# Start and pace of the indirect gathers in a graph layer: which are free at the start, and how often the next is handed over

## The chip, the cores and the metric

One core of one Trainium2 chip runs the whole kernel. The metric is the device time in microseconds (us) of one execution; the median of several runs is compared.

## The reference

The input has 12,500 nodes with 128 features each, and 200,000 edges (source, destination), sorted by destination.

```
h   = maximum(layernorm(x), 0)
agg = segment_sum(h[src], dst) / maximum(deg, 1)
h1  = relu(agg @ Wg + h @ Ws + bg)
h2  = tanh(h1 @ W1 + b1)          # 128 -> 512
h3  = tanh(h2 @ W2 + b2)          # 512 -> 512
out = x + h3 @ W3 + b3            # 512 -> 128
```

## The kernel before

The nodes are cut into 49 blocks of 256. First x is normalized in five chunks; the result is split into a high and a low float16 half, kept in SBUF (`tab`) and written to a table in DRAM (`h_table`). Then the blocks' neighbour sums are made in two ways.

Blocks 0 to 22 ("pool" blocks) are summed from a ring in SBUF. GpSimd issues 744 indirect DMAs, one for each tile of 128 edges, numbered here 0 to 743; each fetches 128 rows of the table into the next of 64 places of the ring (line 638). TensorE multiplies the ring's tiles with one-hot matrices (line 712), 18 tiles for each step of 128 nodes; there are 46 steps, 0 to 45. Before step s, `begin_sums(s)` waits until gathers 0 to 16s + 23 have landed and reads a lead with `value_load`.

Blocks 23 to 48 ("units", 26 of them, 0 to 25) use no gather. For each unit VectorE and TensorE sort the edges into groups (`place_edges`, `count_groups`, `rank_edges`, `spread_ranks`; matmuls of `place_chunk`, line 760, whose result ScalarE copies to `q_sb`, line 1127). TensorE turns the result (line 769), ScalarE copies it to `qlT` (line 1133), and SP writes it to DRAM and spreads it over all partitions (lines 563 and 565, 1.6 MB): these are the unit's codes. VectorE compares the codes with partition numbers (`match_codes`, line 1480), TensorE picks the messages in 25 "pairs" of four matmuls each (`gather_pairs`, line 787), ScalarE copies each pair (line 1113), and `sum_unit` (line 803) adds them up. VectorE's order is written out by hand: at the start it is `rank_edges(0)`, `spread_ranks(0)`, `place_edges(1)`, `count_groups(1)`, `take_nodes(0)` (line 1499, needs `q_sb`), `split_sources(1)`, a memset, and `match_codes(0)`. SP's queue at the start holds the loads of the first three blocks' own rows and then the codes of units 0 and 1.

The dense layers (line 815 and 818 for layer 1, 824, 841, 858 for the others) of one block are interleaved by hand with the pairs of one unit and the sums of two steps. A period takes one pool block and one unit; there are 25 periods, of which 1, 2 and 13 have no pool block's layers.

GpSimd's gathers are released in three ways. The first FIRST_LOTS = 12 wait only for the table. From gather 12 on, the unit 0 codes' `qlT_ready` must have come. From gather OPEN_LOTS = 24 on, each waits for one more increment of `lot_free`. TensorE gives these increments: at each matmul, while the program is built, `pace(mm, ns)` adds an assumed duration to a clock, and if that clock has reached `due` and the ring has a free place, this matmul increments `lot_free`; `due` then moves on by LOT_NS = 1400. These nanoseconds are constants in the code, not measured times. A "lot" is one gather (LOT = 1). After the last step's tiles are in, nothing more is gathered.

Of the kernel before, what the change touches and what calls it, by code (L numbers as in the profile page):

```python
# [35 lines left out]
RING = RG * GT  # L36
RW = 258
LOT = 1
FIRST_LOTS = 12
OPEN_LOTS = 24  # L40
LOT_NS = 1400
BLK = 256
SUB = 128
W = 18
# [25 lines left out]
def at(eng, sem, value):  # L70

    if not isinstance(value, int) or value > 0:
        eng.wait_ge(sem, value)


def wait_alone(eng, sem, value, passed):

    eng.wait_ge(sem, value)
    eng.sem_inc(passed)


def gnn_program(nc, x, src, dst, Wg, Ws, bg, W1, b1, W2, b2, W3, b3, out):
# [61 lines left out]
    with ExitStack() as ctx:  # L144
# [280 lines left out]
        def chunk_rows(c):  # L425

            return TP, ROWS, xin[:, c * ROWS:(c + 1) * ROWS]
# [5 lines left out]
        def table_whole(eng):  # L433
            for s in range(2):
                eng.wait_ge(table_in[s], 16 * len(SPREAD) * ((TC + 1 - s) // 2))
# [14 lines left out]
        def over_all_tiles(eng, m, step):  # L450

            step(0, m * TILES + 1)
            with eng.Fori(1, TILES - 1) as t:
                step(t, m * TILES + t + 1)
            step(TILES - 1, (m + 1) * TILES)

        def is_general(eng):
            eng.wait_ge(general_ready, 1)
            return eng.value_load(general[0:1, 0:1], min_val=0, max_val=1) > 0
# [140 lines left out]
        @block.gpsimd  # L600
        def _(pool):
            nc.gpsimd.memset(ident[:], 0.0).then_inc(ident_zero, 1)
            pool.wait_ge(ident_zero, 1)
            nc.gpsimd.affine_select(out=ident[:], in_=ident[:], compare_op=ALU.not_equal, fill=1.0, base=0,
                                    pattern=[[-1, P]], channel_multiplier=1).then_inc(ident_ready, 1)
            nc.gpsimd.iota(iota, pattern=[[1, BLK]], base=0, channel_multiplier=0,
                           allow_small_or_imprecise_dtypes=True).then_inc(iota_ready, 1)
            pool.wait_ge(ident_ready, 1)
            nc.gpsimd.tensor_copy(ident16[:], ident[:]).then_inc(ident_ready, 1)
            nc.gpsimd.iota(threshold[:], pattern=[[0, 1]], base=0, channel_multiplier=SUB,  # L610
                           allow_small_or_imprecise_dtypes=True).then_inc(iota_ready, 1)
            nc.gpsimd.iota(base_tab[:, 0:STEPS], pattern=[[SUB, STEPS]], base=0, channel_multiplier=0,
                           allow_small_or_imprecise_dtypes=True).then_inc(iota_ready, 1)
            nc.gpsimd.iota(base_tab[:, STEPS:SUBS], pattern=[[SUB, SUBS - STEPS]], base=STEPS * SUB - 1, channel_multiplier=0,
                           allow_small_or_imprecise_dtypes=True).then_inc(iota_ready, 1)
            nc.gpsimd.iota(first_row, pattern=[[16, SUBS]], base=-15, channel_multiplier=0,
                           allow_small_or_imprecise_dtypes=True).then_inc(iota_ready, 1)

            for c in range(TC):
                s = c % 2  # L620
                p, rows, held = chunk_rows(c)
                at(pool, pair_ready, c - 1)
                pool.wait_ge(shift_ready, c + 1)
                for r in range(POOL_ROWS):
                    ins = nc.gpsimd.tensor_scalar(hval[0:p, s, r, 0:D], held[0:p, r], scale[0:p, s, r:r + 1],
                                                  shift[0:p, s, r:r + 1], ALU.mult, ALU.add)
                ins.then_inc(pool_scaled, 1)

            table_whole(pool)
            pool.wait_ge(turned, 2 * TB)  # L630

            pool.wait_ge(idx_turned, TB)

            def gather_lot(d):

                for t in range(LOT * d, LOT * (d + 1)):
                    k = t // GT % RG
                    nc.gpsimd.indirect_dma_start(  # L638
                        out=ring_tiles[:, t % RING, 0:2 * D], out_offset=None, in_=table,
                        in_offset=bass.IndirectOffsetOnAxis(ap=idx_all[:, t:t + 1], axis=0),  # L640
                    ).then_inc(gathered[k], 16)

            for d in range(LOTS):
                if d == FIRST_LOTS:
                    pool.wait_ge(qlT_ready, 1)
                elif d >= OPEN_LOTS:
                    wait_alone(pool, lot_free, d - OPEN_LOTS + 1, issuing)
                gather_lot(d)

            with pool.If(is_general(pool)):  # L650
                def gather_tile(t, n):
                    wait_alone(pool, gen_idx_ready, n, issuing)
                    nc.gpsimd.indirect_dma_start(
                        out=ring_tiles[:, 0, 0:2 * D], out_offset=None, in_=table,
                        in_offset=bass.IndirectOffsetOnAxis(ap=general_idx[:, 0:1], axis=0),
                    ).then_inc(gen_gathered, 16)

                with pool.Fori(0, BLOCKS) as m:
                    pool.sem_inc(gen_counting)
                    over_all_tiles(pool, m, gather_tile)  # L660

                    wait_alone(pool, gen_seg, (m + 1) * TILES, issuing)
                    pool.inc_swdge_sem([gen_gathered], [16 * TILES], mode="sub")

        @block.tensor
        def _(pe):
# [22 lines left out]
            def pace(mm, ns, tells=False):  # L689

                lots["clock"] += ns
                free = min(LOTS, lots["summed"] + LOTS_HELD) - lots["given"] - OPEN_LOTS
                if lots["clock"] >= lots["due"] and free > 0 and not tells:
                    lots["given"] += 1
                    lots["due"] = max(lots["due"] + LOT_NS, lots["clock"] + LOT_NS * 3 // 4)
                    mm.then_inc(lot_free, 1)

            def begin_sums(s):

                assert lots["given"] + OPEN_LOTS >= STEP_LOTS * s + (2 * GT + GT) // LOT  # L700
                at(pe, mean_done, s)
# [148 lines left out]
            def layer4(k, carried=0, beside=None, paced=True):  # L850

                at(pe, oblk_ready, k)
                at(pe, carry_taken, carried)
                for t in range(NT):
                    for q in range(HC):
                        if t == 0 and q in (0, HC - 1):
                            pe.wait_ge(h3_ready, HC * k + (HC if q else HC - 1))
                        mm = nc.tensor.matmul(out_ps[:, t], h3T[:, q, t * P:(t + 1) * P], w3[:, q],  # L858
                                              start=(q == 0), stop=(q == HC - 1))
                        if paced:  # L860
                            pace(mm, 215, t == NT - 1 and q == HC - 1)
                        if t == NT - 1 and q == HC - 1:
                            mm.then_inc(l4_done, 1)
                        if beside:
                            beside(HC * t + q)
# [143 lines left out]
            layer4(LAST_UNIT)  # L1009
            assert lots["given"] == LOTS - OPEN_LOTS  # L1010

# [722 lines left out]
```

## Time and profile before

| | us |
|---|---|
| median of 3 runs | 1424.96 |
| lowest and highest | 1423.08 to 1429.42 |
| the profiled execution | 1426.06 |
| its span, first to last instruction | 1424.1 |
| TensorE matmuls busy | 1238.2 (87%) |
| VectorE busy | 1085.5 (76%) |
| GpSimd busy | 754.2 (53%) |
| ScalarE busy | 628.0 (44%) |

The times in the profile are those of one execution, counted from its first instruction. An engine's idle time is shown before the instruction that ended it, with what released it; "issue" and "remote" mean that no instruction of this core was found as releaser. Ends of matmuls are modelled, their starts are recorded.

### The profile page before, as it was taken

Reading aid. Unit: us, or ns where it says so; the run is one execution under the profiler, and the core shown is the slowest. Engines: PE = TensorE matmul, PEld = TensorE weight load, DVE = VectorE, ACT = ScalarE, POOL = GpSimd, SP = SyncE. Lnnn points to the kernel's source line nnn. Section 1 sums busy time; section 2 is a strip of 40 time slices with the busy share of each in tenths; the row PEclk is TensorE's granted clock in tenths of the full one; section 3 lists DMA queues with packets and bytes.
Section 4 is the critical chain, followed back from the end, with each engine's and each line's share of the span. In section 5 each row is a group of like instructions: output and inputs, shape, how many; then the busy total and the mean of one; then the engine's idle time right before and its main releaser. Section 6 shows DMA issues by size and latency. Waiting matters only on the chain.

```text
span 1424.1 us, 28546 instructions
## 1 busy us (share of the span) xinstructions
PE 1238.2 (87%) x10196; PEld 942.0 (66%) x10196; DVE 1085.5 (76%) x2058; ACT 628.0 (44%) x1297; POOL 754.2 (53%) x796
## 2 busy tenths in 40 slices
PE   0327888999999999999989989999999999999988
PEld 0114666776776777777766767777767777777767
DVE  8787899678778868868867886886787788788641
ACT  6513455345435435435525543553453354354342
POOL 3274644555555555555545555555555565555530
PEclk9658999999999999999999999999999999999999
DMA  9632412441441342342233225324414414423410
GB/s 236 220 111 80 96 45 77 104 110 40 107 109 52 99 104 63 85 107 83 66 101 96 81 63 107 87 62 109 105 44 107 111 44 103 109 65 82 112 32 11
DMA packets 88769, 129.02 MB, mean 91 GB/s; under 512 B 45329, under 2 KB 71271, under 8 KB 84055
## 3 DMA queue, kind: packets, MB, share of 16 engines
q1 hardware_dynamic: 64825, 78.37, 20.5%
q0 software_dynamic: 23808, 48.81, 14.1%
q8 instruction: 88, 1.44, 0.4%
q14 instruction: 48, 0.39, 0.1%
HBM read 107.53 MB, written 13.16 MB: 85 GB/s over the span
## 4 chain that ended last, share of the span: by engine, by line
PE 74%; DVE 8%; issue 6%; ACT 5%; another core or an unknown queue 4%; DMA 3%; DVEq 0%; SPq 0%; POOL 0%; POOLq 0%; ACTq 0%
PE banks L841 22%; PE banks L787 21%; PE banks L803 8%; PE banks L858 6%; PE banks L712 6%; PE banks L824 4%; DVE arena L1490 3%; PE banks L760 2%; ACT arena L1113 2%; DMA xin<-in_x_dram 2%; PE banks L818 2%; PE banks L815 2%; ACT dense L1096 1%; DVE arena L1480 1%
## 5 line engine op out<-in xcount | busy, mean ns | idle before, releaser
L638 POOL DMA_INDIRECT ring<-h_table,idx_all x744 | 732.5, 984 | 588.9 <-issue 221.6
L1113 ACT CAST arena<-banks 128x512 f16<-128x512 f32 x650 | 366.0, 589 | 192.3 <-PE banks L787 141.6
L787 PE MATMUL banks<-xin,arena 125*128 125x256 f16 x2600 | 371.7, 276 | 63.5 <-issue 26.6
L841 PE MATMUL banks<-dense,w 128*128 128x256 f32 (+1 forms) x1568 | 419.0, 384 | 8.7 <-ACT dense L1096 4.7
L787 PEld LDWEIGHTS banks<-xin,arena 125*128 125x128 f16 x2600 | 236.7, 98 | 164.0 <-issue 80.8
L841 PEld LDWEIGHTS banks<-dense,w 128*128 128x128 f32 x1568 | 265.7, 191 | 47.3 <-ACT dense L1096 13.4
L1490 DVE TENSOR_TENSOR arena<-node,banks 128x768 f16<-128x768 f16 x208 | 191.5, 981 | 22.0 <-PE banks L803 21.5
L1480 DVE TENSOR_SCALAR arena<-arena,code_ptr 128x768 f16<-128x768 f16 (+1 forms) x416 | 177.6, 489 | 17.8 <-PE banks L787 14.9
L803 PE MATMUL banks<-arena 64*128 64x257 f16 x2600 | 162.1, 271 | 5.7 <-DVE arena L1490 3.4
L712 PE MATMUL banks<-ring,onehot 128*128 (+1 forms) x828 | 158.5, 274 | 1.1 <-issue 0.2
L1103 ACT ACTIVATE dense<-banks,b2c 128x256 f32<-128x256 f32 (+1 forms) x196 | 93.6, 479 | 130.6 <-PE banks L841 113.2
L803 PEld LDWEIGHTS banks<-arena 64*128 64x128 f16 x2600 | 119.1, 94 | 46.7 <-issue 18.5
L1339 DVE TENSOR_TENSOR onehot<-iota,banks 128x2304 f16<-128x2304 f16 x46 | 117.5, 2554 | 1.6
L824 PE MATMUL banks<-dense,w 128*128 128x256 f32 (+1 forms) x392 | 109.5, 396 | 8.0 <-ACT dense L1088 8.0
L1551 DVE TENSOR_TENSOR dense<-banks,xblk 128x256 f32<-128x256 f32 x49 | 20.8, 425 | 123.2 <-issue 60.4
L858 PE MATMUL banks<-w,dense 128*128 128x128 f32 x784 | 111.4, 283 | 2.9 <-DMA ring<-h_table,idx_all 1.7
L712 PEld LDWEIGHTS banks<-ring,onehot 128*128 128x128 f16 x828 | 78.7, 97 | 52.4 <-issue 14.2
L1096 ACT ACTIVATE dense<-banks,b1c 128x256 f32<-128x256 f32 (+1 forms) x196 | 81.9, 470 | 65.9 <-PE banks L824 55.4
L858 PEld LDWEIGHTS banks<-w,dense 128*128 128x128 f32 x784 | 100.0, 191 | 14.2 <-issue 9.3
L1433 DVE TENSOR_TENSOR arena<-arena,banks 128x1800 f16<-128x1800 f16 x52 | 102.9, 2021 | 0.1
L1088 ACT ACTIVATE dense<-banks,bgc 128x256 f32<-128x256 f32 (+1 forms) x49 | 23.2, 474 | 164.4 <-PE banks L818 153.5
L824 PEld LDWEIGHTS banks<-dense,w 128*128 128x128 f32 x392 | 67.8, 196 | 21.5 <-ACT dense L1088 15.3
(123 smaller groups left out, 862.8 us busy)
## 6 DMA issues: line engine op xcount, KB each, us to landing
arena<-unit_codes SPq DMA_DIRECT2D x26, 1600.0 KB
ring<-h_table,idx_all POOLq DMA_INDIRECT x744
xblk<-in_x_dram SPq DMA_DIRECT2D x48, 128.0 KB
out_dram<-dense SPq DMA_DIRECT2D x48, 128.0 KB
xin<-in_x_dram SPq DMA_DIRECT2D x5, 1120.0 KB
h_table<-xin SPq DMA_DIRECT2D x5, 1120.0 KB
own_pair<-h_table SPq DMA_TRANSPOSE x98
w<-in_L_gnn_W_dram SPq DMA_DIRECT2D x1, 1024.0 KB, 11.5
```

Source lines behind the costliest of these rows:

```text
L638: nc.gpsimd.indirect_dma_start(out=ring_tiles[:, t % RING, 0:2 * D], out_offset=None, in_=table, in_offset=bass.IndirectOffsetOnAxis(ap=id ...
L712: mm = nc.tensor.matmul(main_ps[:, 0:2 * D + 1], onehot[:, s % 2, j, :], ring_column(window_slot(s, lead, j)), start=(j == 0), stop=(j == ...
L787: mm = nc.tensor.matmul(to, wide_l[0:TP, piece % WSLOTS, k, j, :], tab[0:TP, row_of(g, j), :], start=(j == 0), stop=(j == 1))
L803: mm = nc.tensor.matmul(unit_ps[h][:, 0:2 * D + 1], wide[h * HALF:(h + 1) * HALF, (NP + p) % WSLOTS, g - lo, 0:P], unit_msgs[h * HALF:(h + ...
L824: mm = nc.tensor.matmul(l2_ps[c][:, 0:w], w1[:, c * P:(c + 1) * P], h1T[:, 0:w], start=True, stop=True)
L841: mm = nc.tensor.matmul(l3_ps[c][:, 0:w], w2[:, q, c * P:(c + 1) * P], h2T[:, q, 0:w], start=(q == 0), stop=(q == HC - 1))
L858: mm = nc.tensor.matmul(out_ps[:, t], h3T[:, q, t * P:(t + 1) * P], w3[:, q], start=(q == 0), stop=(q == HC - 1))
L1113: nc.scalar.copy(unit_msgs[:, 2 * pr:2 * pr + wide_of, 0:2 * D], unit_ps[pr % 2][:, 0:wide_of * 2 * D].rearrange("p (g d) -> p g d", d=2 * ...
L1339: nc.vector.tensor_tensor(onehot[:, b], iota16[:].unsqueeze(1).to_broadcast([P, W, P]), held.unsqueeze(2).to_broadcast([P, W, P]), ALU.is_ ...
L1433: ins = nc.vector.tensor_tensor(oh_pay[:, :, k], hits[:, :, 0:HI], place_ps[:, 1 + k].unsqueeze(2).to_broadcast([P, UT, HI]), ALU.mult)
L1480: ins = nc.vector.tensor_scalar(wide_l[:, p % WSLOTS, 0:hi - lo, j, :], codes[:, lo * P:hi * P].rearrange("p (g w) -> p g w", w=P), code_p ...
L1490: nc.vector.tensor_tensor(wide[:, (NP + p) % WSLOTS, 0:hi - lo, 0:P], node16[:, 0:P].unsqueeze(1).to_broadcast([P, hi - lo, P]), qd_ps[:, ...
```

## The change

The first gather of all now waits for `qlT_ready`, the copy that unit 0's codes are written from. Only 14 gathers are then free in place of 24; every later one is handed over by TensorE's `pace`, whose interval is 1375 in place of 1400 ns. FIRST_LOTS is gone. The number of increments rises from 720 to 730.

```diff
-FIRST_LOTS = 12
-OPEN_LOTS = 24
-LOT_NS = 1400
+OPEN_LOTS = 14
+LOT_NS = 1375
...
             for d in range(LOTS):
-                if d == FIRST_LOTS:
+                if d == 0:
                     pool.wait_ge(qlT_ready, 1)
-                elif d >= OPEN_LOTS:
+                if d >= OPEN_LOTS:
                     wait_alone(pool, lot_free, d - OPEN_LOTS + 1, issuing)
                 gather_lot(d)
```

## Rows read from the trace of the kernel before

**Rows 1.** First section of the page: busy us, share of the span, instructions.

```profile
PE 1238.2 (87%) x10196; PEld 942.0 (66%) x10196; DVE 1085.5 (76%) x2058; ACT 628.0 (44%) x1297; POOL 754.2 (53%) x796
```

**Rows 2.** Groups by line: busy, mean ns, idle before and its releaser.

```profile
L638 POOL DMA_INDIRECT ring<-h_table,idx_all x744 | 732.5, 984 | 588.9 <-issue 221.6
...
L712 PE MATMUL banks<-ring,onehot 128*128 (+1 forms) x828 | 158.5, 274 | 1.1 <-issue 0.2
```

**Rows 3.** Timeline of GpSimd at the start: start, duration, idle before.

```profile
71.78 1.14 POOL L638 DMA_INDIRECT ring<-h_table,idx_all  x1 [20.85 <-DMA h_table<-xin]
...
85.93 1.34 POOL L638 DMA_INDIRECT ring<-h_table,idx_all  x1 [0.30 <-issue]
90.61 1.22 POOL L638 DMA_INDIRECT ring<-h_table,idx_all  x1 [3.35 <-ACT qlT L1133]
...
112.32 0.94 POOL L638 DMA_INDIRECT ring<-h_table,idx_all  x1 [0.31 <-issue]
116.14 0.95 POOL L638 DMA_INDIRECT ring<-h_table,idx_all  x1 [2.87 <-PE banks L787]
```

**Rows 4.** Timeline of TensorE's matmuls at the start.

```profile
82.09 0.96 PE L760 MATMUL banks<-arena 128*64 128x100 f16 x18 [0.30 <-DVE arena L1458]
...
99.95 7.15 PE L787 MATMUL banks<-xin,arena 125*128 125x256 f16 x36 [9.91 <-DVE arena L1480]
108.92 0.60 PE L787 MATMUL banks<-xin,arena 125*128 125x256 f16 x4 [1.82 <-issue]
110.29 0.61 PE L787 MATMUL banks<-xin,arena 125*128 125x256 f16 x4 [0.77 <-issue]
113.83 1.04 PE L787 MATMUL banks<-xin,arena 125*128 125x256 f16 x4 [2.93 <-issue]
116.05 1.01 PE L787 MATMUL banks<-xin,arena 125*128 125x256 f16 x4 [1.19 <-ACT arena L1113]
...
117.28 8.98 PE L787 MATMUL banks<-xin,arena 125*128 125x256 f16 x48
126.94 1.01 PE L760 MATMUL banks<-arena 128*64 128x100 f16 x36 [0.68 <-ACT arena L1113]
...
135.00 0.28 PE L712 MATMUL banks<-ring,onehot 128*128 128x257 f16 x1
```

**Rows 5.** Timeline of ScalarE at the start.

```profile
89.27 0.24 ACT L1127 COPY q_sb<-banks 128x100 f32<-128x100 f32 x1 [17.46 <-remote]
...
113.19 0.59 ACT L1113 CAST arena<-banks 128x512 f16<-128x512 f32 x1 [2.96 <-remote]
...
127.99 0.24 ACT L1127 COPY q_sb<-banks 128x100 f32<-128x100 f32 x1 [1.10 <-PE banks L760]
```

**Rows 6.** Timeline of VectorE at the start.

```profile
86.48 0.37 DVE L1413 TENSOR_TENSOR arena<-arena 128x400 f16<-128x400 f16 x1
89.55 0.21 DVE L1499 COPY banks<-q_sb 128x50 f32<-128x50 f32 x1 [2.69 <-ACT q_sb L1127]
...
97.47 0.10 DVE L1664 MEMSET arena<- 128x50 f16 x1 [0.24 <-DVE code_all L1328]
98.82 2.96 DVE L1480 TENSOR_SCALAR arena<-arena,code_ptr 128x768 f16<-128x768 f16 x8 [1.25 <-DMA arena<-unit_codes]
```

**Rows 7.** Chain that ended last, in order of time: start, us, what.

```profile
90.37 1.29 DMA unit_codes<-qlT
91.67 6.64 DMA arena<-unit_codes
...
1371.33 2.51 DMA ring<-h_table,idx_all
```

**Rows 8.** Timeline of TensorE's matmuls, end of the last two periods.

```profile
1321.04 0.59 PE L818 MATMUL banks<-dense,wg 128*128 128x256 f32 x2
...
1372.49 0.59 PE L818 MATMUL banks<-dense,wg 128*128 128x256 f32 x2
1374.84 0.68 PE L858 MATMUL banks<-w,dense 128*128 128x128 f32 x4 [1.75 <-DMA ring<-h_table,idx_all]
```

## The prediction

> **What bounds the kernel now.** The page's first section comes first: TensorE is busy 1238.2 of 1424.1 us and GpSimd, which only issues the gathers, 754.2 [rows 1]. The middle of the kernel is matmul after matmul, so a change of the gathers can pay only where TensorE sits idle. Next the groups by line: the 744 gathers stood idle 588.9 us in total, so GpSimd is not the limit, and the matmuls that read the gathered tiles (L712) lost 1.1 us to waiting [rows 2]. That leaves the timeline at the two ends of the gather stream, engine by engine.
>
> The head. GpSimd issues gathers 0 to 11 in one run from 71.78 to 85.93, waits for unit 0's codes, and issues 12 to 28 in a second run to 112.32; from 116.14 on it waits for matmuls [rows 3]. Beside the first run, the 36 matmuls of place_chunk(0) end at 82.09 + 0.96 = 83.05, yet ScalarE's copy of their result starts at 89.27, after 17.46 us of waiting [rows 4, 5]. For unit 1 the same pair of steps has no gap: matmuls end at 126.94 + 1.01 = 127.95, copy at 127.99. So **6.2 us** are lost before 89.27. Beside the second run TensorE's pairs lose 1.82 + 0.77 + 2.93 + 1.19 = **6.7 us** between 107 and 116 [rows 4], and ScalarE's cast at 113.19 waited 2.96 us [rows 5] though its matmuls, pair 9's, ended at 108.92 + 0.60 = 109.52. Once gathers are paced, 48 matmuls take 8.98 us from 117.28 without a gap [rows 4]. Late completions thus lie beside long gather runs. Against that, the first 36 pair matmuls (pairs 0 to 8), 7.15 us from 99.95, lie in the second run and have no such gap.
>
> The tail. Step 45 needs the very last gather, issued at 1371.33 and landed 2.51 us later [rows 7]. TensorE had ended layer 1 at 1372.49 + 0.59 = 1373.08 and starts at 1374.84: **1.75 us** idle [rows 8].
>
> **The change part by part.**
>
> *First gather behind unit 0's codes.* Nothing is queued behind the waiting gather on GpSimd but other gathers. It empties 71.8 to 90 of twelve gathers. If these caused the 6.2 us, ScalarE's copy starts at 83.1. What is late next is VectorE: it finishes count_groups(1) at 86.48 + 0.37 = 86.85; take_nodes(0), split_sources and the memset took 89.55 to 97.57, 8.02 us [rows 6], so they would end at 94.9. The codes, 6.2 us earlier on SP, would land at 91.67 + 6.64 - 6.2 = 92.1 [rows 7] and no longer matter. match_codes(0) then starts at 95.0 in place of 98.82 [rows 6]: **-3.8 us**, not 6.2. The cover for the other 2.4 is VectorE's own work.
>
> Here a rule speaks against the gain. The trace shows a late completion beside gathers, no mechanism [rows 3, 4]. The Trainium skill, "SBUF — State Buffer", section "Who interferes with whom", says a DMA never contends with a compute engine. By it the 6.2 us stay, and the sum loses its 3.8. The first-run gap speaks against this rule here and the 36 undisturbed matmuls for it.
>
> *14 free in place of 24, all others handed over.* The run after the codes is 14 gathers, plus those that pace() has handed over by then. Adding up pace()'s own ns along TensorE's program: gathers 14 and 15 go in place_chunk(0), then one each 1375 ns, which is 3 pairs. Gathers cost 1.26 us each (85.93 - 71.78 over 11, 1.29) [rows 3]; from 84.4 on, gather 14 is reached at 102.4 and 20 at 110, when pair 14 (the one that hands it over) is due at 96.1 + 14 x 0.8 = 107 (0.8 is 7.15 over 9 pairs) [rows 4]. So the long run now ends at about 110 after 20 gathers, in place of 29, but still lies beside the pairs. The 6.7 us can vanish (-6.7), stay (0) or grow (D). The row nearest to the new order is the old second run itself, which had the loss: I take 0.
>
> Ten more gathers wait for a semaphore; paced and unpaced ones are both issued 0.30 us after the last when free [rows 3], so this costs 0.
>
> Is the ring filled in time? Step 0 needs gather 23. By the same adding up it is handed over at 12.5 us of pace clock, in pair 23 of unit 0, near 117.28 + 8.98 - 0.6 = 125.7 today. With 0.95 to issue and at most 2.51 to land it is there at 128.3; step 0 starts at 135.00 [rows 4, 7]. Both ends move together, so 6.7 us are spare: cost 0, and if that cover is gone, its excess. Step 1 needs gather 39, handed over at 34.9 us of pace clock where the step begins at 46.8: also 0.
>
> *1375 in place of 1400 ns.* At step 43 the last gather needed is handed over at 1026.2 us of pace clock before and 1011.4 after; for step 45 it is 1073.4 and 1057.8, of 1075.1 when the step begins. Between those steps, layer 1 ends move from 1321.04 to 1372.49, 51.45 us, for 44.7 of pace clock, so 15.6 is 18 us of time [rows 8]. The last gather would be in the ring about 16 us before its use: **-1.75 us**, all of it on the path, since only matmuls follow. Nothing else waits there; no gain is to be had at other steps, where L712 hardly waits [rows 2]. The steeper pace adds no DMA bytes.
>
> Sum: -3.8 - 1.75 = -5.55 on an execution of 1426.06 (span 1424.1 and 2.0 around it), 1420.5. The three times have their median at 1424.96, 1.1 below, so the median after is **1419.4**, 0.39% less.
>
> **Rivals.**
>
> A (forecast, 0.40): as above, 1419.4.
>
> B (0.25): both losses come from long runs of gathers, and the shorter second run takes away its loss too. For it: the pairs from 117.28 on are clean as soon as gathers are paced. Against: 20 gathers in a row remain beside or before them. 1424.96 - 5.55 - 6.7 = 1412.7.
>
> C (0.20): the first gap isn't the gathers' doing, so the change does nothing at the head; tail gain only, 1423.2. For it: the ends of matmuls are the profile's model, and pairs 0 to 8 ran undisturbed beside gathers. Against: units 0 and 1 run the same 36 matmuls and only one is late. On this the Trainium skill, "Perfetto Trace Analysis", section "Tensor Engine Instruction (MATMUL, LD_WEIGHTS)", says the end shown for a matmul is an estimate and the semaphore follows PSUM's acknowledgement; taken alone it would leave the gap unexplained but real, at C's time.
>
> D (0.10, slower): the run now begins ten gathers before the pairs, and holds TensorE's completions from the first pair until about the run's end, as the first run held place_chunk(0)'s until 89.27, 2 us after its last gather. Sixteen gathers from 84.4 are issued by 104.6 and landed by 107. Pair 12 would then start at 107 + 11 x 0.8 = 115.8, against 116.05 today: the head's gain is gone but for 0.2. If the last three of today's gaps come on top, 0.77 + 2.93 + 1.19 = 4.9 are lost: 1424.96 - 0.2 + 4.9 - 1.75 = 1427.9. It is slower than before once pair 12 starts later than 116.05 + 1.75 = 117.8. Gather 23 would have to be 6.7 us late to add to this.
>
> The rest (0.05): small shifts of the phases of the periods, either way, 2 us.
>
> **How the numbers follow.** The three times spread over 6 us, and 0.5% is 7.1 us: that is what I take as telling a change from none, so faster means below 1417.8, slower above 1432.1. Faster: B, 0.25, and what of A (a partial gain in the pairs, over 1.6 of the 6.7) and the rest falls below the line, 0.09: 0.34. Slower: D prolonged by another 4.2 us or with gather 23 late: 0.06. Same: 0.60. Range: from B less 1.7 us of scatter to between C and D: 1411 to 1426, leaving out D's end and the edges. A's own range is 1417 to 1422.
>
> **What the profile after would show.** Step 1: ScalarE's q_sb copy (L1127) at about 83 and the first gather just after 84; else C. Step 2: VectorE at work without a gap from 82 to 95 and L787 starting near 96. Step 3: gathers back to back up to number 20 or so, then waiting for L787; gaps in L787 of about 6.7 us in total for A, none for B, over 10 for D. Step 4: step 0 starts near 131 with no wait for the ring. Step 5: the last gather near 1350, and L858 of step 45 starts 0.1 to 0.4 us after L818 ends. The prediction is wrong if q_sb's copy stays near 89, or if the middle, from 140 to 1320, changes its length by more than 2 us, where I expect nothing.

## The result, and the profile after

The changed kernel takes **1441.0 us** (median of 11 runs) against 1425.61 us of the kernel before beside it: a ratio of **1.0099, 95% interval 1.008 to 1.0118**. It is slower by 1%, where 1419.4 us, 0.4% faster, was predicted. The ratio leaves out one run of each kernel, 2087.29 us at a granted clock of 0.562, and 1807.06 us. The profiled execution took 1435.4 us, with a span of 1433.5 us; it is 9.3 us longer than the profiled one of the kernel before (1426.06), while the medians lie 15.4 us apart, so the two profiles show some 60% of the loss. In what follows lines of the changed kernel are one lower than before (L786 is the pairs' L787).

First section of the page after, and the groups by line (busy, mean ns, idle before and its releasers):

```profile
PE 1240.8 (87%) x10196; PEld 942.8 (66%) x10196; DVE 1082.7 (76%) x2058; ACT 625.4 (44%) x1297; POOL 746.3 (52%) x796
```

```profile
L786 PE MATMUL banks<-xin,arena 125*128 125x256 f16 x2600 | 370.7, 276 | 84.2 <-ACT arena L1112 39.8 <-DVE arena L1479 23.8 <-issue 17.9
L1112 ACT CAST arena<-banks 128x512 f16<-128x512 f32 x650 | 365.1, 590 | 217.8 <-PE banks L786 178.3 <-issue 21.3 <-remote 12.6
L802 PE MATMUL banks<-arena 64*128 64x257 f16 x2600 | 167.4, 271 | 11.9 <-DVE arena L1489 6.6 <-issue 3.8
L857 PE MATMUL banks<-w,dense 128*128 128x128 f32 x784 | 111.4, 283 | 0.4 <-issue 0.3
```

The busy times are within 8 us of those before [rows 1]. TensorE's idle time grew by 6.8 us, from 1424.1 - 1238.2 = 185.9 to 1433.5 - 1240.8 = 192.7. In the pairs and their casts it grew by more: these two groups had 63.5 us (L787) and 192.3 us (L1113) of it in the kernel before, and have 84.2 and 217.8 now; other groups have less than before.

**The head came out as predicted.** Timelines of ScalarE, VectorE, GpSimd and TensorE at the start (four fences in this order; ... marks lines left out):

```profile
83.05 0.24 ACT L1126 COPY q_sb<-banks 128x100 f32<-128x100 f32 x1 [11.28 <-PE banks L759]
...
110.32 0.59 ACT L1112 CAST arena<-banks 128x512 f16<-128x512 f32 x1 [2.92 <-remote]
```

```profile
86.69 0.20 DVE L1498 COPY banks<-q_sb 128x50 f32<-128x50 f32 x1
...
94.45 0.44 DVE L1479 TENSOR_SCALAR arena<-arena,code_ptr 128x768 f16<-128x768 f16 x1
```

```profile
85.07 1.14 POOL L637 DMA_INDIRECT ring<-h_table,idx_all  x1 [34.78 <-ACT qlT L1132]
...
110.78 0.95 POOL L637 DMA_INDIRECT ring<-h_table,idx_all  x1 [0.31 <-issue]
114.75 1.32 POOL L637 DMA_INDIRECT ring<-h_table,idx_all  x1 [3.02 <-PE banks L786]
```

```profile
82.04 0.96 PE L759 MATMUL banks<-arena 128*64 128x100 f16 x18 [0.30 <-DVE arena L1457]
...
95.50 8.31 PE L786 MATMUL banks<-xin,arena 125*128 125x256 f16 x44 [11.69 <-DVE arena L1479]
105.33 0.61 PE L786 MATMUL banks<-xin,arena 125*128 125x256 f16 x4 [1.52 <-ACT arena L1112]
107.54 1.01 PE L786 MATMUL banks<-xin,arena 125*128 125x256 f16 x4 [1.60 <-issue]
...
110.96 1.03 PE L786 MATMUL banks<-xin,arena 125*128 125x256 f16 x4 [1.99 <-issue]
113.09 1.03 PE L786 MATMUL banks<-xin,arena 125*128 125x256 f16 x4 [1.09 <-issue]
...
131.44 1.74 PE L711 MATMUL banks<-ring,onehot 128*128 128x257 f16 x14
```

The q_sb copy follows its matmuls at 83.05. Twenty gathers run back to back from 85.07 to 110.78. The four gaps in the pairs sum to 1.52 + 1.60 + 1.99 + 1.09 = 6.2 us, where 6.7 us was expected to stay. Step 0 starts at 131.44, 3.6 us before the 135.00 of [rows 4].

**The tail too.** TensorE at the last step: the wait of 1.75 us in [rows 8] is gone.

```profile
1383.27 0.59 PE L817 MATMUL banks<-dense,wg 128*128 128x256 f32 x2
1383.75 0.68 PE L857 MATMUL banks<-w,dense 128*128 128x128 f32 x4
```

**The middle did not.** Start of the last matmul of `sum_unit(n)`, us:

| unit | before | after | difference |
|---|---|---|---|
| 0 | 134.8 | 131.2 | -3.6 |
| 3 | 272.2 | 271.3 | -0.9 |
| 8 | 531.0 | 535.1 | +4.1 |
| 15 | 884.2 | 887.0 | +2.8 |
| 22 | 1242.6 | 1255.2 | +12.6 |
| 24 | 1346.2 | 1358.9 | +12.7 |
| 25 | 1387.6 | 1396.5 | +8.9 |

So 12.7 + 3.6 = **16.3 us** were lost between units 0 and 24, in small pieces: 2.7 to unit 3, 5.0 from there to unit 8, -1.3 to unit 15, 10.0 to unit 24. What a piece looks like, in unit 6 of the changed kernel: GpSimd, then ScalarE.

```profile
393.72 0.95 POOL L637 DMA_INDIRECT ring<-h_table,idx_all  x1 [1.80 <-issue]
394.97 0.95 POOL L637 DMA_INDIRECT ring<-h_table,idx_all  x1 [0.30 <-issue]
396.23 0.95 POOL L637 DMA_INDIRECT ring<-h_table,idx_all  x1 [0.30 <-issue]
397.48 1.13 POOL L637 DMA_INDIRECT ring<-h_table,idx_all  x1 [0.31 <-issue]
398.91 0.95 POOL L637 DMA_INDIRECT ring<-h_table,idx_all  x1 [0.30 <-issue]
400.17 0.95 POOL L637 DMA_INDIRECT ring<-h_table,idx_all  x1 [0.30 <-issue]
```

```profile
394.96 0.59 ACT L1112 CAST arena<-banks 128x512 f16<-128x512 f32 x1 [0.29 <-PE banks L786]
395.83 1.07 ACT L1112 CAST arena<-banks 128x512 f16<-128x512 f32 x2 [0.29 <-PE banks L786]
...
397.96 0.59 ACT L1112 CAST arena<-banks 128x512 f16<-128x512 f32 x1 [0.68 <-PE banks L786]
399.42 0.59 ACT L1112 CAST arena<-banks 128x512 f16<-128x512 f32 x1 [0.88 <-PE banks L786]
400.84 0.59 ACT L1112 CAST arena<-banks 128x512 f16<-128x512 f32 x1 [0.83 <-PE banks L786]
402.29 1.07 ACT L1112 CAST arena<-banks 128x512 f16<-128x512 f32 x2 [0.87 <-PE banks L786]
```

Six gathers run with 0.30 us between them. Before the casts beside the first two ScalarE is idle for 0.29 us, before those beside the later ones for 0.68 to 0.88 us. It looks like the loss of the head again, in small, in the middle.

**Late time.** To add this up I use one measure for all profiles. A pair's late time is the start of ScalarE's cast, less the later of two times: 0.25 us after the start of the pair's last matmul, and 0.53 us after the cast before it. Over 650 pairs it is 121.5 us in the kernel before, with 57 pairs over 0.75 us, and 139.0 us in the changed one, with 76. The difference, 17.5 us, has the size of the loss. Stretch by stretch the two agree only roughly: the late time differs by -1.2 us in units 1 to 3, +11.4 in 4 to 8, +1.9 in 9 to 15 and +6.6 in 16 to 24.

### The profile page after: what moved, and what is told of

Read it like the earlier page. It is cut to its first block, busy times and chain, and to the rows that moved or that the text cites. A ratio compares the mean times of both kernels' runs of the same rounds, so it can differ in the third digit from the quotient of the medians.

```text
span 1433.5 us, 28556 instructions
## 1 busy us (share of the span) xinstructions
PE 1240.8 (87%) x10196; PEld 942.8 (66%) x10196; DVE 1082.7 (76%) x2058; ACT 625.4 (44%) x1297; POOL 746.3 (52%) x796
## 4 chain that ended last, share of the span: by engine, by line
PE 74%; DVE 13%; issue 5%; ACT 4%; DMA 2%; another core or an unknown queue 2%; DVEq 0%; SPq 0%
PE banks L840 22%; PE banks L786 21%; PE banks L802 7%; PE banks L857 7%; PE banks L711 6%; DVE arena L1489 5%; PE banks L823 3%; ACT arena L1112 2%; PE banks L814 2%; DMA xin<-in_x_dram 2%; PE banks L759 2%; PE banks L817 2%; DVE arena L1479 1%; PE banks L736 1%
## 5 line engine op out<-in xcount | busy, mean ns | idle before, releaser
L637 POOL DMA_INDIRECT ring<-h_table,idx_all x744 | 724.6, 974 | 592.9 <-issue 192.2
L1112 ACT CAST arena<-banks 128x512 f16<-128x512 f32 x650 | 365.1, 590 | 217.8 <-PE banks L786 178.3
L786 PE MATMUL banks<-xin,arena 125*128 125x256 f16 x2600 | 370.7, 276 | 84.2 <-ACT arena L1112 39.8
L786 PEld LDWEIGHTS banks<-xin,arena 125*128 125x128 f16 x2600 | 236.3, 98 | 187.1 <-issue 63.6
L802 PE MATMUL banks<-arena 64*128 64x257 f16 x2600 | 167.4, 271 | 11.9 <-DVE arena L1489 6.6
L1550 DVE TENSOR_TENSOR dense<-banks,xblk 128x256 f32<-128x256 f32 x49 | 20.8, 424 | 153.7 <-issue 80.8
L823 PEld LDWEIGHTS banks<-dense,w 128*128 128x128 f32 x392 | 68.8, 199 | 16.9 <-ACT dense L1087 10.1
```

The source lines that it names most:

```text
L637: nc.gpsimd.indirect_dma_start(out=ring_tiles[:, t % RING, 0:2 * D], out_offset=None, in_=table, in_offset=bass.IndirectOffsetOnAxis(ap=id ...
L786: mm = nc.tensor.matmul(to, wide_l[0:TP, piece % WSLOTS, k, j, :], tab[0:TP, row_of(g, j), :], start=(j == 0), stop=(j == 1))
L802: mm = nc.tensor.matmul(unit_ps[h][:, 0:2 * D + 1], wide[h * HALF:(h + 1) * HALF, (NP + p) % WSLOTS, g - lo, 0:P], unit_msgs[h * HALF:(h + ...
L823: mm = nc.tensor.matmul(l2_ps[c][:, 0:w], w1[:, c * P:(c + 1) * P], h1T[:, 0:w], start=True, stop=True)
L1112: nc.scalar.copy(unit_msgs[:, 2 * pr:2 * pr + wide_of, 0:2 * D], unit_ps[pr % 2][:, 0:wide_of * 2 * D].rearrange("p (g d) -> p g d", d=2 * ...
```

## The experiments

Eighteen runs were made, in seven groups; each group shared a chip and its runs of the kernel before. The difference between the chips turned out to be the main thing that they showed. Below, a pair is called late when its late time is over 0.75 us, and a chip is said to have late pairs when its profiles show them. All chips but D were used in one group only, so nothing here tells a trait of the chip from something else that was so at that time, such as work on its other cores; on D all groups gave the same.

| chip | kernel before, us | runs |
|---|---|---|
| that of the result | 1425.61 | the kernels before and after |
| B | 1442.9 | after_1385, before_1375, before_wait_first, after_12_early |
| C | 1324.32 | before_again, after_join, after_pairs_slow, after_pairs_fast |
| D | 1324.2 | before_second, after_second, after_join_second, after_pairs_slow_second |
| D | 1325.03 | no_gathers, after_pairs_slow_third, after_join_third |
| E | 1448.52 | no_gathers_second |
| F | 1323.66 | after_pairs_slow_fourth |
| D | 1324.23 | after_join_fourth |

### Each part alone (chip B)

Three theories are held against each other. P: what counts is which matmuls hand over the gathers. Adding up pace's own ns, 281 of 730 increments sit on a pair's matmul in the changed kernel, 127 of 720 in the kernel before, and 134 of 730 at an interval of 1385. R: the shorter interval itself costs, by its size. F: the late start of the gathers costs. The changed kernel itself did not run on this chip.

**after_1385.**

```diff
-LOT_NS = 1375
+LOT_NS = 1385
```

> The changed kernel with one number altered, LOT_NS 1385 in place of 1375. Adding up pace()'s nanoseconds along the program, 281 of the changed kernel's 730 increments sit on a pair's matmul (127 of 720 before); with 1385 it is 134 of 730, at nearly the same interval and with the same start. Theory P (where the increments fall in the program sets how often a gather is issued beside a pair, and that costs the 13 us of the middle): the middle is as before, the head gain of 3.6 us and the tail gain stay, so 1418 to 1423 and a ratio of 0.995 to 0.999. Theory R (the shorter interval itself costs, by its size): 10 of the 25 ns are given back, ratio 1.005 to 1.007. Theory F (the late start and the emptier ring cost): ratio 1.01 as the changed kernel.

Measured: 1453.33 us, ratio to before 1.0074 [1.0052, 1.0097]. P's forecast fell: with about as few increments on pairs as in the kernel before, it is no faster for it. The interval takes in R's 1.007 and F's 1.01.

**before_1375.** The kernel before with the interval alone:

```diff
-LOT_NS = 1400
+LOT_NS = 1375
```

> The kernel before with only LOT_NS changed to 1375: 24 free, first gather as before; 278 of 720 increments on a pair's matmul. Theory P: the whole middle loss and no head gain, ratio 1.010 to 1.014. Theory R: the same. Theory F: no loss, ratio 0.998 to 1.001 with the tail gain of 1.75 us.

Measured: 1453.35 us, 1.0063 [1.0039, 1.0087]. So on this chip the interval alone costs 0.6%, where F forecast no loss and P and R 1.0 to 1.4%.

**before_wait_first.** The kernel before with the wait moved alone; 24 gathers are free behind the codes:

```diff
-                if d == FIRST_LOTS:
+                if d == 0:
                     pool.wait_ge(qlT_ready, 1)
-                elif d >= OPEN_LOTS:
+                if d >= OPEN_LOTS:
```

> The kernel before with only the wait moved to gather 0 (24 free, 1400 ns kept). Theories P and R: the head gain of 3.6 us and nothing else, ratio 0.996 to 0.999; step 0 starts near 131.4. Theory F: a loss, ratio above 1.003.

Measured: 1451.91 us, 1.006 [1.004, 1.008]. This is the mechanism of rival D of the prediction, in the kernel before. TensorE in unit 0's pairs:

```profile
106.59 0.61 PE L787 MATMUL banks<-xin,arena 125*128 125x256 f16 x4 [2.17 <-issue]
110.22 1.01 PE L787 MATMUL banks<-xin,arena 125*128 125x256 f16 x4 [3.02 <-issue]
...
113.71 1.03 PE L787 MATMUL banks<-xin,arena 125*128 125x256 f16 x4 [2.06 <-issue]
120.05 1.03 PE L787 MATMUL banks<-xin,arena 125*128 125x256 f16 x4 [5.30 <-issue]
129.29 6.00 PE L787 MATMUL banks<-xin,arena 125*128 125x256 f16 x27 [8.22 <-ACT arena L1113]
```

The pairs start 4 us earlier than in [rows 4], and then lose 2.17 + 3.02 + 2.06 + 5.30 + 8.22 = 20.8 us beside one run of 30 gathers, from 85.53 to 123.61, where the kernel before loses 6.7. The last matmul of `sum_unit(0)` starts at 146.1, against 135.8 in before_1375, which starts its gathers as the kernel before does. These 10.3 us at the head are the size of the whole loss, 1451.91 - 1442.9 = 9.0.

**after_12_early.** The changed kernel, with the wait at gather 12:

```diff
-                if d == 0:
+                if d == 12:
                     pool.wait_ge(qlT_ready, 1)
```

> The changed kernel (14 free, 1375 ns) with the wait for unit 0's codes back at gather 12, so that 12 gathers go at once. Theories P and R: the middle loss stays and the head gain goes, ratio 1.011 to 1.014, and the copy of q_sb is back at about 89. Theory F: most of the loss goes, ratio 1.000 to 1.005.

Measured: 1450.05 us, 1.0048 [1.0027, 1.0069]. Its unit 0 is clean. GpSimd and TensorE:

```profile
95.37 1.25 POOL L637 DMA_INDIRECT ring<-h_table,idx_all  x1 [0.30 <-issue]
103.44 0.94 POOL L637 DMA_INDIRECT ring<-h_table,idx_all  x1 [6.82 <-PE banks L786]
105.85 1.01 POOL L637 DMA_INDIRECT ring<-h_table,idx_all  x1 [1.48 <-PE banks L786]
```

```profile
90.13 0.47 PE L768 MATMUL banks<-ident,q_sb 128*128 128x128 f32 x1 [6.84 <-ACT q_sb L1126]
100.33 4.94 PE L786 MATMUL banks<-xin,arena 125*128 125x256 f16 x24 [9.72 <-DVE arena L1479]
...
110.05 7.75 PE L786 MATMUL banks<-xin,arena 125*128 125x256 f16 x48
```

The first gap is back (6.84 us of waiting for q_sb, beside gathers 0 to 11), since these gathers run early again. The run ends at gather 15, before the pairs, and the 25 pairs have a late time of 1.9 us in all, against 10.0 in the kernel before, 11.2 in the changed one and 25.2 in before_wait_first. So single gathers about 2 us apart beside the pairs cost little; runs of them cost. It is slower than the kernel before all the same. (Its profile is of its fastest execution, 1440.32 us.)

**Head and middle apart.** The table gives where each profile has the last matmul of `sum_unit(0)`, and the length from there to that of unit 24. The last column moves this length by median less profiled execution; it is an estimate.

| kernel | chip | interval | unit 0 at | units 0 to 24 | profiled | median | estimate |
|---|---|---|---|---|---|---|---|
| before | of the result | 1400 | 134.8 | 1211.4 | 1426.06 | 1425.61 | 1211 |
| after | of the result | 1375 | 131.2 | 1227.7 | 1435.4 | 1441.0 | 1233 |
| before_wait_first | B | 1400 | 146.1 | 1227.8 | 1453.86 | 1451.91 | 1226 |
| before_1375 | B | 1375 | 135.8 | 1249.7 | 1460.82 | 1453.35 | 1242 |
| after_1385 | B | 1385 | 131.4 | 1243.2 | 1450.28 | 1453.33 | 1246 |
| after_12_early | B | 1375 | 129.3 | 1235.9 | 1440.32 | 1450.05 | 1246 |

On both chips the kernels with the shorter interval have the longer middle, wherever their gathers start: by 8 to 22 us as profiled. The moved wait with 24 free gathers costs at the head and not in the middle. So the loss in the middle goes with the new interval, and not by its size (R), since 1385 costs as much as 1375. The late time of the pairs does not show it on chip B: outside unit 0 it is 130.9 us in before_wait_first and 125.4 to 140.2 us in the other three. Each row is one execution, and there is no profile of the kernel before on chip B: its head is taken to be that of before_1375, and its middle that of before_wait_first.

### Another start with the old schedule, and other intervals beside the pairs (chip C)

Theory G: completions are late beside gathers, and the placement in the middle sets how many. E: the late start costs later, whatever the schedule. (The expectation of after_pairs_slow says that pairs over 1.0 us behind a gather were late by under 0.1 us. That holds for their mean, not for each: where no gather was issued from 1.0 us before to 0.6 us after a pair's last matmul, the mean is 0.06 us and the most 0.41 in the kernel before.)

**before_again** is the kernel before, for its profile on this chip.

> The kernel before, unchanged, for its profile on this chip: the one profile that the others of this group are to be held against. No theory speaks here.

Measured: 1329.9 us in its one run; the 27 runs beside it have a median of 1324.32. That is 7 to 8% under the two chips before it.

**after_join.** The changed kernel's start, then the kernel before's schedule (computed beside its own, with 24 and 1400):

```diff
+                old = lots["clock"] >= lots["old_due"] and free > lots["old"] + 24 and not tells
...
+                if old if lots["joined"] else own:
                     lots["given"] += 1
...
+                if lots["given"] + OPEN_LOTS == lots["old"] + 24:
+                    lots["joined"] = True
...
+            lots["gap"] = 1000
             for c in range(UCH):
                 place_chunk(1, c)
```

> The head of the changed kernel (first gather behind unit 0's codes, 14 free, 1375 through unit 0's pairs), then an interval of 1000 until as many gathers are handed over as in the kernel before, and from there on the kernel before's own schedule, matmul for matmul. Theory G (the loss in the middle comes from which matmuls hand over the gathers, and so from how many gathers are issued beside the pairs): the middle is the kernel before's again and the head keeps its 3.6 us: ratio 0.996 to 0.999. Theory E (the later start leaves something behind, a shorter lead of the gathers or another phase of the periods, that costs later whatever the schedule is): ratio 1.003 to 1.010, with the head's gain lost by unit 8.

**after_pairs_slow.**

```diff
-LOT_NS = 1375
+LOT_NS = 1100
+BESIDE_NS = 2000
...
                 for pr in pairs:
+                    lots["gap"] = BESIDE_NS
...
                     mm.then_inc(pair_done, 1)
+                    if pr == PAIRS - 1:
+                        lots["gap"] = LOT_NS
```

> The changed kernel with two intervals in place of one: 2000 while the pairs of a unit run, 1100 elsewhere. By adding up pace's own ns, 266 of 730 gathers are then handed over while pairs run, in place of 363. Theory G: late completions of pairs lie beside an issued gather in every profile so far (a pair whose last matmul starts more than 1.0 us after the last gather's issue began was late by under 0.1 us), so about a quarter of the late time, 139 us in the changed kernel's profile, goes, some 35 us, and of that 0.7 reaches the end: 15 to 30 us faster than the changed kernel, ratio to the kernel before 0.985 to 0.998. Theory E: the ring is no fuller for it, ratio 1.005 to 1.015, or more where the gathers of a step now come too late.

**after_pairs_fast** has the same edit with LOT_NS = 1700 and BESIDE_NS = 1150.

> The opposite: 1150 while the pairs of a unit run, 1700 elsewhere, which hands over about 410 of 730 gathers while pairs run, in place of 363. Theory G: late time up by an eighth, 17 us, 10 us slower than the changed kernel, ratio to the kernel before 1.012 to 1.022. Theory E: as the changed kernel, 1.008 to 1.012.

Measured: after_join 1323.48 us, 0.9999 [0.9983, 1.0014]; after_pairs_slow 1323.05, 1.0002 [0.9982, 1.0022]; after_pairs_fast 1320.98, 0.9985 [0.9969, 1.0001]. Neither theory's numbers. None of the four profiles has one pair late by over 0.75 us; the late time over 650 pairs is 17 us in each. On this chip the placement of gathers makes no difference that these runs can tell, and G and E can't be told apart.

### The kernels before and after on chip D

> The kernel before again, for its profile on this group's chip. What the last group showed is that chips differ: there the kernel before took 1324 us and not one of its 650 pairs was late by over 0.75 us, where the profile it was predicted from has 57 such pairs at 1426 us. If that is the difference between the chips, a chip near 1425 to 1445 us shows 50 to 70 late pairs again, and a chip near 1324 none.

> The changed kernel, unchanged. Theory G (the loss is late completions of pairs beside gathers): on a chip with late pairs ratio 1.005 to 1.012, on a chip without them 0.997 to 1.0005, with the head 2 to 4 us shorter, the tail's wait gone, and the middle the same within 2 us. Theory E (the later start costs by itself): 1.005 to 1.012 on either chip.

Measured: before_second 1323.45 us in one run, no late pair. **after_second 1320.9 us against 1324.2, ratio 0.998 [0.9967, 0.9993].** The same change that costs 1% on the chip of the result gains 0.2% here. The groups by line of before_second, then its ScalarE and GpSimd at the start:

```profile
L1113 ACT CAST arena<-banks 128x512 f16<-128x512 f32 x650 | 360.6, 590 | 138.1 <-PE banks L787 128.6 <-issue 4.2
L787 PE MATMUL banks<-xin,arena 125*128 125x256 f16 x2600 | 358.3, 274 | 27.0 <-DVE arena L1480 25.6 <-ACT arena L1113 1.0
```

```profile
83.41 0.24 ACT L1127 COPY q_sb<-banks 128x100 f32<-128x100 f32 x1 [11.28 <-PE banks L760]
```

```profile
82.50 0.94 POOL L638 DMA_INDIRECT ring<-h_table,idx_all  x1 [0.30 <-issue]
83.75 0.94 POOL L638 DMA_INDIRECT ring<-h_table,idx_all  x1 [0.30 <-issue]
85.00 0.94 POOL L638 DMA_INDIRECT ring<-h_table,idx_all  x1 [0.30 <-issue]
```

The pairs waited 27.0 us in all, against 63.5 for the same program in the profile that the prediction read. The copy comes at 83.41 in the middle of the first run of gathers: the 6.2 us of the head are not there to be gained. Only the tail's wait is, and it goes. TensorE's last step in before_second, then in after_second:

```profile
1270.02 0.59 PE L818 MATMUL banks<-dense,wg 128*128 128x256 f32 x2
1272.38 0.68 PE L858 MATMUL banks<-w,dense 128*128 128x128 f32 x4 [1.77 <-DMA ring<-h_table,idx_all]
```

```profile
1268.74 0.59 PE L817 MATMUL banks<-dense,wg 128*128 128x256 f32 x2
1269.37 0.68 PE L857 MATMUL banks<-w,dense 128*128 128x128 f32 x4
```

Between the sums' ends of units 3 and 24 the two profiles keep the same distance, -0.9 to -1.3 us: here the middle does not change its length, as predicted. At unit 25 it is -3.0.

**after_join_second, after_pairs_slow_second**, the kernels of the last group again:

> The changed kernel's head with the kernel before's schedule from the end of unit 0's pairs on, again. On a chip with late pairs theory G gives 0.996 to 1.000, theory E 1.003 to 1.010. On a chip without them 0.999 to 1.001, as in the last group.

> The changed kernel with 2000 while pairs run and 1100 elsewhere, again. On a chip with late pairs theory G gives 15 to 30 us less than the changed kernel, ratio to before 0.985 to 0.998; theory E 1.005 to 1.015. On a chip without them both give 0.999 to 1.001.

Measured: 1324.56 us, 1.0007 [0.9993, 1.002], and 1324.74 us, 1.0001 [0.9988, 1.0014]. No difference again.

### No gathers (chips D and E)

The kernel before with 72 gathers in place of 744; from step 4 on TensorE sums what stands in the ring:

```diff
-            for d in range(LOTS):
+            for d in range(4 * STEP_LOTS + 8):
...
-                for g in range(2 * s + 1 if s else 0, 2 * s + 3):
+                for g in range(2 * s + 1 if s else 0, 2 * s + 3) if s < 4 else ():
```

> The kernel before with gathers 0 to 71 only: the other 672 are left out, and from step 4 on TensorE sums what stands in the ring, without waiting. The output is another one for it. Theory G (late completions come from gathers beside them): on a chip with late pairs there are none after unit 3, and the time falls to that of the chips without them, 1320 to 1335 us, ratio 0.92 to 0.94. Rival K (completions are late on such a chip whatever GpSimd does, the gathers only lie everywhere): 50 or more pairs stay late and the ratio is 0.99 to 1.00. On a chip without late pairs both give 0.995 to 1.00, where a gain would be the tail's wait for the last gather, 1.7 us.

Measured on chip D: 1317.27 us against 1325.03, 0.9929 [0.9906, 0.9952]. The 672 gathers cost 8 us there, more than the tail's wait and more than the 0.5% that was expected at most, and this chip's profiles have no late pair to put it down to. Held against before_second's, the profile is 1.8 us behind at unit 3, 3.1 ahead at unit 24 and 5.2 ahead at unit 25: 4.9 us come in small steps over the middle, then the tail. What makes the small steps is not known.

> The kernel before with gathers 0 to 71 only, the other 672 left out; the output is another one for it. On a chip with late pairs (before at 1400 us or more) theory G: no late pair after unit 3, time 1310 to 1335 us, ratio 0.91 to 0.94; rival K: 50 or more late pairs, ratio 0.985 to 1.00. On a chip without them both 0.990 to 0.996, as the last group measured.

Measured on chip E: **1333.41 us against 1448.52, ratio 0.9203 [0.9179, 0.9226].** This is theory G's case, and K falls. Its groups by line, beside [rows 1, 2]:

```profile
L1113 ACT CAST arena<-banks 128x512 f16<-128x512 f32 x650 | 361.2, 590 | 143.9 <-PE banks L787 122.9 <-issue 12.2 <-remote 3.8
L787 PE MATMUL banks<-xin,arena 125*128 125x256 f16 x2600 | 360.5, 274 | 34.4 <-DVE arena L1480 23.1 <-ACT arena L1113 6.4 <-issue 4.4
```

The late time by unit is 10.1, 3.0 and 2.9 us for units 0 to 2, the ones beside the 72 gathers, and 0.6 us for each later one. Held against the same kernel's profile on chip D, it is 14.7 us behind at the end of unit 3 and 13.8 us behind at the end of unit 25. It is 0.6 us behind when the first gather is issued, 72.68 us against 72.10. So nearly all that chip E loses in this kernel, it loses while gathers run. The runs do not tell the issuing of the gathers by GpSimd from their traffic. The first gap is there as well; ScalarE at the start on chip E:

```profile
90.32 0.24 ACT L1127 COPY q_sb<-banks 128x100 f32<-128x100 f32 x1 [17.63 <-remote]
```

### Still the placement

> The changed kernel with 2000 while pairs run and 1100 elsewhere. On a chip with late pairs theory G gives a ratio to before of 0.985 to 0.998, theory E (the later start costs by itself) 1.003 to 1.015. On a chip without them both 0.998 to 1.001.

> The changed kernel's head with the kernel before's schedule from the end of unit 0's pairs on. On a chip with late pairs theory G gives 0.996 to 1.000, theory E 1.003 to 1.010. On a chip without them both 0.999 to 1.001.

> The changed kernel with 2000 while pairs run and 1100 elsewhere. On a chip with late pairs (before at 1400 us or more): without gathers such a chip gains 115 us, so the 27% fewer gathers beside pairs should be worth up to 30 us: theory G gives a ratio to before of 0.980 to 0.998 and fewer than 60 late pairs. Rival S (gathers make completions late, but what counts is not how many lie beside the pairs; elsewhere they delay other completions as much): ratio 1.002 to 1.015, as every other variant on such a chip. On a chip without late pairs 0.998 to 1.001.

> The changed kernel's head with the kernel before's schedule from the end of unit 0's pairs on. On a chip with late pairs (before at 1400 us or more): if the new schedule is the cause, 0.996 to 1.000; if it is the later start, 1.003 to 1.010. On a chip without late pairs 0.999 to 1.001, for either.

Measured, all on chips without late pairs: 1324.98 us, 0.9996 [0.9979, 1.0013]; 1323.69, 0.9993 [0.9979, 1.0007]; 1325.61, 1.0005 [0.9986, 1.0025]; 1325.2, 1.0005 [0.9993, 1.0017]. They confirm that nothing moves there, and leave the question of the placement open on chips with late pairs.

## Why the prediction was wrong

**The step that failed** is the third of the change part by part, "1375 in place of 1400 ns", with the ring's schedule before it. It priced the new hand-overs by two things only: is the ring filled in time, and does the last gather come earlier. It asked where the change can pay, and left the middle at nothing, with the words "where I expect nothing". What the runs showed in its place: the middle grew by 16.3 us. The interval alone, in before_1375, costs 0.6% on chip B, and the table of heads and middles puts that loss between units 0 and 24 in each kernel with the shorter interval. Behind it lies that on such a chip gathers are not free for the pairs in any period: late time is 111.5 us outside unit 0 in the kernel before, and 127.8 us in the changed one, where chips C and D have 17 us in all.

The reading that would have warned stood in the prediction itself. It took the late completions for a thing of the head's two long runs, because 48 paced matmuls from 117.28 ran without a gap. That was a stretch of one period, chosen where it was clean. The groups by line of the kernel before had the rest:

```profile
L787 PE MATMUL banks<-xin,arena 125*128 125x256 f16 x2600 | 371.7, 276 | 63.5 <-issue 26.6 <-DVE arena L1480 17.1 <-ACT arena L1113 16.7
L1113 ACT CAST arena<-banks 128x512 f16<-128x512 f32 x650 | 366.0, 589 | 192.3 <-PE banks L787 141.6 <-issue 35.2 <-remote 9.9
```

Of L787's idle time 26.6 us are "issue", and of L1113's 35.2 us "issue" and 9.9 us "remote": waits whose end no recorded instruction explains. In before_second, on chip D, the cast's "issue" is 4.2 us, and "remote" is not among the releasers shown.

**Step by step.** Steps 1, 2 and 4: right, the copy at 83.05, VectorE without a gap, step 0 at 131.44 for 131. Step 3: right in sort and size, 20 gathers in the run and 6.2 us of gaps against 6.7; case A at the head, not B. Step 5: right in that the wait is gone, on two chips; the last gather is issued at 1366.88 and not near 1350, which is 16.9 us before its use at 1383.75, as forecast, since the use itself moved. The head's -3.8 measured -3.6. The two terms of the sum are right for where they lie; the loss lies between them. (In the time of gather 23, 125.7 + 0.95 + 2.51 is 129.2 and not 128.3, which leaves 5.8 us spare in place of 6.7; the term stays 0.)

**The rivals.** C came out on chip D, the only one without late pairs where the changed kernel ran, for another reason than it gave: there no gap stands beside the first gathers, and the ratio is 0.998, its tail gain and about 1 us more. D, at 0.10, was the one rival with a slower kernel, and had the right kind of mechanism and the wrong place: with 24 gathers free (before_wait_first) the head lost 10.3 us more; with 14 free it stayed as forecast, and the time of 1441.0 lies far above D's 1427.9.

On this the Trainium skill, "SBUF — State Buffer", section "Who interferes with whom", says that a DMA never contends with a compute engine. The engines' instructions are indeed hardly slower: a pair matmul takes 276 ns with late completions and 274 without. On chip D no pair is late beside gathers, and leaving out 672 of them gave 0.7%. On chip E it gave 8%, so as a rule for when work can start it does not hold there; the measurement decides.

**What the loss in the middle hangs on.** From the two profiles, pairs of units 1 to 25 by how many gathers were issued in the 5.6 us around the start of the pair's last matmul (5.0 before it, 0.6 after):

| gathers near | pairs, before | mean late, us | pairs, after | mean late, us |
|---|---|---|---|---|
| 2 or fewer | 61 | 0.03 | 98 | 0.03 |
| 3 | 282 | 0.14 | 287 | 0.09 |
| 4 or more | 282 | 0.25 | 240 | 0.41 |

In before_second and after_second 437 and 433 pairs have four or more near, and their mean late time is 0.02 us. So lateness grows with how closely the gathers follow each other, and only where there are late pairs at all. The changed kernel has fewer crowded pairs, and each is later. after_1385 shows that the loss is not in how many increments stand on pairs (134 there, 281 in the changed kernel). That crowding is what the shorter interval changed is argued from these rows, and no experiment shows it. It fits after_12_early, where gathers 2 us apart left unit 0 clean.

**What stays open.** By which mechanism a shorter interval lengthens the middle on a chip with late pairs, since the pairs' late time follows it only in part; whether the changed start with the old schedule would keep its 3.6 us there; and whether wider intervals beside the pairs would gain there. Both kernels for it ran four times and came to chips without late pairs each time. What makes the chips differ was not found. No version that beats both kernels on every chip was found either: on chip D the changed kernel is the better by 0.2%, on the chip of the result the kernel before by 1%.

## What to carry to other kernels

A gap beside a long run of background DMAs may be a price that they have everywhere, so look for it over the whole kernel before moving their schedule: add up the idle time with no releaser ("issue", "remote") of the consumers of the busiest engine. The gap that a schedule is tuned against may be there on some chips only: measure on more than one, and read an effect of under 1% as one of the chip that it was measured on until another shows it. Take head, middle and tail apart in each profile, since two kernels with the same total can lose in different places. The cheapest test of whether background traffic costs anything is a kernel that leaves it out.

## What the runs showed of the hardware that was not expected

- The same program takes 1324 us on three chips and 1425 to 1449 us where completions are late, 8 to 9% more, at the same granted clock (0.969 in the profile of before and in that of before_again) and with nearly the same busy times of ScalarE (628.0 and 622.3 us) and VectorE (1085.5 and 1085.3). TensorE's is 1238.2 against 1206.7 us. That is mostly not slower matmuls: pair matmuls overlap, 2600 of 276 ns cover 371.7 us, and of 274 ns 359.2 us.
- Where completions are late, the indirect DMAs or their issuing make them so: without 672 of 744 gathers chip E's time fell by 115 us, 0.17 us for each gather left out, and late time fell to 0.6 us per unit.
- The gathers themselves do not take longer on such a chip: by the DMA records, the median of the 744 landed 2.25 us after its issue began in the profile of before, and 2.26 us in that of before_second.
- Beside a run of 30 gathers TensorE stood idle for up to 8.22 us before one pair (before_wait_first), while gathers about 2 us apart left 25 pairs with a late time of 1.9 us in all (after_12_early).
